# Macaron layer on one core: new call sequences on all engines before and after the loop over the attention units

## What is computed

```python
x = x + 0.5 * ffn(layernorm(x))
x = x + attention(layernorm(x))
x = x + 0.5 * ffn(layernorm(x))
```

```python
logits = flat @ router_w.T
_, topk_idx = top_k(logits + router_bias, 4)
topk_w = softmax(logits) at topk_idx, divided by its sum
y = einsum(silu(xg @ gate) * (xg @ up), down)     # xg: the tokens of each expert
out = zeros.at[tok_table].add(y * w_table)        # scatter-add
out = out + shared experts of flat
```

```python
q, k, v = x @ (codes * scales) + bias
attn = softmax(q @ k.T / sqrt(128))
out = (attn @ v) @ (wo_codes * wo_scales) + bo
```

## Time and profile before

| what | us |
|---|---|
| median of 3 runs | 972.84 (972.01 to 973.99) |
| profiled execution | 972.94 |
| its span, first to last instruction | 971.2 |
| PE matmul busy | 915.0 (94%) |
| VectorE busy | 763.6 (79%) |
| ScalarE busy | 646.6 (67%) |
| GpSimd busy | 645.6 (66%) |
| mean granted TensorE clock | 0.988 |

### The profile page before, as it was taken

One profiled execution on the slowest core, in us unless ns is written; L12 is line 12 of the kernel. 1 busy time (PEld: TensorE's weight loads), 2 busy tenths in 40 slices (PEclk: granted clock), 3 DMA queues, 4 the chain that ended last, 5 costly groups with the idle time before them and its releaser, 6 DMA issues.

```text
span 971.2 us, 18502 instructions
## 1 busy us (share of the span) xinstructions
PE 915.0 (94%) x5770; PEld 561.1 (58%) x5772; DVE 763.6 (79%) x2079; ACT 646.6 (67%) x1426; POOL 645.6 (66%) x607
## 2 busy tenths in 40 slices
PE   4999789999999999999999999999999999978987
PEld 3766466555555555555555555555555555765666
DVE  6954399998888888888888888888878789876247
ACT  5634446877778687777778778777777787543431
POOL 3368778878676868778676766867677455236741
PEclk9999989999999999999999999999999999988999
DMA  8979745666765868797785766756575564485757
GB/s 338 356 247 316 270 163 163 100 136 109 153 129 101 169 151 185 141 223 158 177 192 98 153 104 137 153 103 140 107 151 96 90 120 87 89 334 153 250 204 273
DMA packets 302978, 165.58 MB, mean 170 GB/s; under 512 B 278176, under 2 KB 285600, under 8 KB 300832
## 3 DMA queue, kind: packets, MB, share of 16 engines
q1 hardware_dynamic: 297696, 146.56, 62.7%
q0 software_dynamic: 3072, 9.44, 3.0%
q10 hardware_dynamic: 2112, 8.39, 2.1%
HBM read 68.93 MB, written 28.31 MB: 100 GB/s over the span
## 4 chain that ended last, share of the span: by engine, by line
PE 75%; DVE 13%; DMA 4%; issue 3%; ACT 2%; SPq 1%; another core or an unknown queue 0%; POOL 0%; DVEq 0%; ACTq 0%
PE b_p L110 5%; PE b_o L110 5%; PE b_o L111 5%; PE b_o L112 5%; PE b_p L111 5%; PE b_p L112 5%; PE b_s L110 5%; PE b_s L112 5%; PE b_s L111 5%; PE b_out L110 3%; PE b_out L112 3%; PE b_out L111 3%; PE b_v L110 2%; PE b_v L112 2%; PE b_v L111 2%
## 5 line engine op out<-in xcount | busy, mean ns | idle before, releaser
L2452 POOL TENSOR_TENSOR h<-pr,h 128x512 f16<-128x512 f32 x256 | 293.1, 1158 | 160.6 <-ACT h L1171 155.1
L1161 ACT ACTIVATE pr<-b_s,nmax,kappa 128x512 f32<-128x512 f32 x256 | 197.5, 774 | 41.1 <-DVE nmax L1907 36.7
L1904 DVE TENSOR_SCALAR_CACHE_REDUCE junk<-b_s 128x512 bf16<-128x512 f32 x256 | 175.3, 685 | 22.6 <-PE b_s L112 17.5
L1171 ACT ACTIVATE h<-pr 128x512 f16<-128x512 f32 x256 | 153.3, 626 | 0.7 <-DMA pT<-h 0.4
L1935 DVE SCALAR_TENSOR_TENSOR x<-b_out,rinv,x 128x256 f32<-128x256 f32 x256 | 111.4, 476 | 41.8 <-PE b_out L112 40.3
L110 PE MATMUL b_p<-xh,w 128*128 128x512 f16 x256 | 97.8, 382 | 3.1 <-DVE qT L1846 2.2
L110 PE MATMUL b_o<-pT,v 128*128 128x512 f16 x256 | 97.1, 379 | 1.7 <-DVE oT L1923 1.7
L111 PE MATMUL b_p<-xh,w 128*128 128x512 f16 x256 | 97.8, 382 | 0.0
L110 PE MATMUL b_s<-kT,qT 128*128 128x512 f16 x256 | 97.1, 379 | 0.7 <-ACT pr L1161 0.7
L112 PE MATMUL b_p<-xh,w 128*128 128x512 f16 x256 | 97.6, 381 | 0.0
L111 PE MATMUL b_s<-kT,qT 128*128 128x512 f16 x256 | 97.1, 379 | 0.0
(11 more groups left out here) (223 smaller groups left out, 2234.1 us busy)
## 6 DMA issues: line engine op xcount, KB each, us to landing
raw<-in_experts SPq DMA_DIRECT2D x32, 768.0 KB, 8.0
raw_cs<-in_heads SPq DMA_DIRECT2D x16, 1024.0 KB, 5.2
zrows<-zero ACTq DMA_DIRECT2D x4, 2048.0 KB, 11.5
z<-zrows SPq DMA_DIRECT2D x16, 512.0 KB, 4.2
zrows<-zero SPq DMA_DIRECT2D x16, 512.0 KB, 3.9
zl<-zrows SPq DMA_DIRECT2D x16, 512.0 KB, 8.8
rows<-xn SPq DMA_DIRECT2D x8, 512.0 KB, 10.7
pT<-h SPq DMA_TRANSPOSE x256, 3.2
```

Of the source, the lines that this page charges most:

```text
L1161: act.activation(pr[n % 4][:], b_s[n % 3][:], ACT.Exp, bias=nmax[:, u % 2, i:i + 1], scale=kappa[:, s:s + 1], accum_out=rsum[:, u % 2, i:i ...
L1171: act.activation(h[n % 4][:, 0, :], pr[n % 4][:], ACT.Copy).then_inc(q["p_high"], 1)
L1904: dve.tensor_scalar(junk[n % 2][:], b_s[n % 3][:], 0.0, None, ALU.add, ALU.max, accum_out=peaks[:, n % 2:n % 2 + 1]).then_inc(q["peak_read ...
L2452: pool.tensor_tensor(h[n % 4][:, 1, :], pr[n % 4][:], h[n % 4][:, 0, :], ALU.subtract).then_inc(q["p_split"], 1)
```

## The change

The function bodies, their waits, the buffers and the work are the same. Only the lists of calls change, on all five engines, before the loop and after it; the loops stay as they are. Every call of before is there once, in another place of the list. The diff has some 2,150 lines; these are the parts that the prediction speaks of.

ACT, start of the program (`job(j)` makes the high part of the router's, gate, up and down weights; `zero_out` issues a DMA of 2 MB of zeros):

```diff
             job(0)
             normalise(0)
+            normalise(1)
+            zero_out(0)
+            high(0)
             job(1)
-            high(0)
-            normalise(1)
+            job(2)
+            job(3)
             logits_out(0)
-            job(2)
             normalise(2)
+            normalise(3)
             high(1)
-            zero_out(0)
-            job(3)
-            normalise(3)
             high(2)
+            zero_out(1)
```

SP, start:

```diff
             load_x(0)
             load_x(1)
+            load_x(2)
+            load_qk_bias()
             load_router()
+            load_x(3)
+            load_gate()
             load_up()
-            load_x(2)
-            load_gate()
-            load_x(3)
+            load(0)
             load_down()
-            load(0)
-            load_qk_bias()
-            load_out_bias()
             load(1)
             load(2)
-            load(3)
-            load(4)
             store_rows(0)
             store_rows(1)
             store_rows(2)
             load_qk(0)
+            load(3)
+            load(4)
```

DVE, end of lap 0 (the combines; `scales(0)` and `statistics(4)` lead to the attention):

```diff
             hidden(11)
+            add_shared(1)
             combine(0)
+            combine(1)
             hidden(12)
-            scales(0)
-            combine(1)
             combine(2)
             combine(3)
+            combine(4)
+            scales(0)
             statistics(4)
+            add_shared(2)
             hidden(13)
+            combine(5)
             shift(4)
-            combine(4)
-            combine(5)
+            combine(6)
+            combine(7)
+            statistics(5)
             low(4)
             hidden(14)
-            add_shared(2)
             hidden(15)
-            combine(6)
+            keys_of(0)
             queries(0)
-            keys_of(0)
-            combine(7)
-            statistics(5)
+            shift(5)
             maxima(0, 0)
+            values(0)
```

POOL, the same place:

```diff
             range_weights(0, 2)
+            high_weights(0, 2)
+            power(4)
+            combine(8)
+            low_weights(0, 2)
+            hidden_low(12)
+            hidden_low(13)
+            power(5)
             range_weights(0, 3)
-            high_weights(0, 2)
-            low_weights(0, 2)
+            combine(9)
+            hidden_low(14)
             high_weights(0, 3)
+            hidden_low(15)
             low_weights(0, 3)
-            power(4)
+            combine(10)
...
             scale_weights(1, 0)
             scale_weights(1, 1)
-            hidden_low(12)
-            hidden_low(13)
-            combine(8)
-            hidden_low(14)
-            hidden_low(15)
-            combine(9)
-            combine(10)
-            power(5)
```

```diff
             load_z(28)
             load_z(29)
             load_z(30)
+            load_z(31)
             store_x(0)
-            load_z(31)
             store_x(1)
```

1155 lines of the change are left out of this document (576 added, 579 removed).

## The result

| kernel | median us | runs | ratio to before | granted clock, profiled run |
|---|---|---|---|---|
| before | 973.06 (972.01 to 974.39) | 8 | | 0.988 |
| changed | 980.25 (976.83 to 985.77) | 8 | 1.0077 [1.0051, 1.0103] | 0.992 |

The changed kernel is slower by 0.77%, 7.2 us, and outside the range on record (965.0 to 975.5). Its runs lie in three clusters, 976.8 to 978.4, 979.7 to 980.8 and 985.5 to 985.8. They go with the granted clock of the whole run: 0.992, 0.987 and 0.979. A straight line through the 8 runs gives 972.5 us plus 0.62 times the lost clock (one minus the clock, times the time), and leaves 0.5 us. The profiled run is the fastest of them, 976.83 (span 975.1), 3.9 us over the profiled run of before. So its trace shows about half of the loss, at a clock (0.992) that is even above that of before's profile (0.988); the rest must be read from other runs.

What follows compares the result with a forecast made beforehand. PE was taken to bound the loop, leaving at most the other 400 us to move. Terms +0.9 + 0 − 2.1 − 1.5 + 0 − 0.3 = −3.0 took 972.94 to 969.9 us; range 965.0 to 975.5.

Steps and rivals of the forecast that it cites:

- What bounds the kernel: PE bounds the loop from 250 to 800 us; the change leaves it alone, so at most the other 400 us move.
- A: Start up to the first logits: later down weights delay `logits_out(0)`, less `low_job(3)` taken off DVE's path; +0.9 us.
- B: Experts of both laps: same work in nearly the same order; 0 us, ends ±1.5.
- C: Combine stage: DVE's combines clear of POOL, first scores at 147.4 against 149.5; −2.1 us, ends −6 and +1.
- some 1.3 of collisions: Within the combine stage: time that `combine(6)` and `combine(7)` lose beside POOL, on top of their 3.1 us.
- 3 x 1.3: Combine stage: PE's `keys_of(0)`, `queries(0)` and `keys_of(1)`, 1.3 us each, ahead of the first scores.
- turns reversed: Rival: at the combines, DVE's steps wait for POOL's and `low(4)` ends near 149.7; total 976.4 us, chance 0.20.
- D: Units 1 to 8: DVE enters some 5 us earlier, PE's 3.5 idle us the ceiling; −1.5 us, ends 0 and −3.5.
- E: Units 57 to 63 and lap-1 routers: DVE's savings are waited away; 0 us, ends −2.2 and +1.2.
- F: Tail: `load_z(31)` issued one store earlier; −0.3 us, ends −1 and 0.
- lock rule: DVE and POOL lock their shared port for whole instructions; `combine(5)` and `combine(8)` then run one after the other, 4.3 us.

Runs made afterwards that it cites:

- only_units: The kernel before with the new order from `combine(0)` to unit 7 alone: 977.03 us, 1.0026 of before.
- turns_only: The kernel before with only DVE's and POOL's turns at the combines new, units 1 to 7 as before: 975.40 us, 1.0004 of before.
- Only_end: The kernel before with the new order only behind the loop: 974.57 us, 0.9993 of before.
- only_start: The kernel before with the new order only up to the first experts: 975.16 us, 1.0005 of before.
- before again: The kernel before, unchanged, run again for a second profile: 973.91 us, 0.9987 of before.

## Why the prediction was wrong

**What bounds the kernel**: right. The loop moved by 0.2 us of PE work, and everything happened in the other 400 us.

**A, the start** (+0.9 at the mask and experts, bounds -0.9 to +2.2): right in mechanism. The forecast had `logits_out(0)` at up to 19.9, it came at 19.66, and what it waited for is the down weights, as written. At the mask of chunk 3 it was +1.34, as the `low_job(3)` removed from that path gave back 0.6 and not 1.2. The down weights took 12.2 us to land and not 10.1, with `load(0)` ahead on SP's queue and the zeros of ACT's queue beside. *DMA: Bandwidth & Descriptors* of the Trainium skill, "Issuing engines are not separate DMA queues", says that DMAs of different engines run on the same 16 DMA engines and interleave. The longer landing fits that, but does not show it: no run parts the zeros from `load(0)`, whose 1.9 us by themselves would nearly do.

**B, the experts** (0): right alone (0.9992); +0.4 in the profile.

**C, the combine stage** (-2.1): wrong in sign. It measured +1.1 us in the profile (+2.7 at the scores of unit 0, of which 1.6 was already there at `combine(0)`). `statistics(4)`, `gate_up(14)`, the turn and `shift(4)` came within 0.6 us of the forecast once the 0.9 of the start is added. Two steps failed. One is "some 1.3 of collisions": `combine(6)` and `(7)` lost 2.8 us, so the low part of chunk 4 ended at 146.0 (143.5 plus 0.9 expected). The other is "3 x 1.3": PE's three calls up to the scores were taken at full clock, and took 6.05 us, from 146.17 to 152.22, as the clock was halved for 3.4 of them. The rival "turns reversed" named this place and these collisions; it put the bound at 145.6. It had 0.20, and the median is above even its 976.4. It did not name the clock or the units behind, so it would have been right in part only.

**D, units 1 to 8** (-1.5, bounds -3.5 to 0): the largest miss. It measured +2.1 us in the profile, outside my bounds; by the times of only_units and turns_only, 1.0026 and 1.0004, it is about 2.1 us as well. I had priced it as PE's idle time, a ceiling of 3.5 us that could only shrink, and had put a loss at nothing without a reason. PE's idle time grew to 5.25 us, nearly all of the growth at `values(3)`, and the clock was halved behind that wait. I had not asked what POOL's combines would then stand beside: `combine(14)` stood beside `scales_qk(1)` before, now `combine(13)` does too, and the chain became 1.0 us longer. Nor had I asked what PE has to do while it waits: two `scores` less. turns_only, which leaves this stretch as before, has no loss that can be told.

**E and F** (0 and -0.3): right in size. From unit 55 to `gate_up(31)` the gap fell by 0.4 us, with `shift(11)` and the mask at 0.16 and 0.42 us as forecast, though the turn of chunk 11 came 1.4 us later against unit 55 and not 0.1 to 0.6. From there to the end it fell by 0.5, as the last load's wait at PE's final sums fell. The two lines, of before and of the changed kernel:

```profile
956.11 1.10 PE L389 MATMUL tb<-zl,twice 128*128 128x256 f32 x4 [0.89 <-DMA zl<-zrows]
```

```profile
959.98 1.32 PE L389 MATMUL tb<-zl,twice 128*128 128x256 f32 x5 [0.22 <-DMA zl<-zrows]
```

**The clock** was no term of the sum, and it should have been. Taking 0.6 us per microsecond of lost clock, the slope of the changed kernel's runs, it is at equal clock about 4 us slower than before (972.7 against 968.6 on the chip where both were run again), and its lower clock (0.987 against 0.990 in the medians) adds some 1.8 us; between its own best and worst runs the clock makes 7 to 8 us. The slope is rough: over the other kernels it lies between 0 and 0.9. Of the lock rule of *SBUF — State Buffer* in the Trainium skill ("SBUF: two separate sides"), the trace again shows the kind: a step of 0.16 us waits up to 1.07 us beside a POOL operation of 1.26. The 4.3 us that the prediction gave `combine(5)` and `combine(8)` by that rule came out at 3.6, from 133.28 to 136.85: the two overlap in part.

**What stays open.** The parts measured alone add up to 1.5 us by the ratios, 3 by the medians, on the faster chips; the whole gave 7.2 and 5.9. The clock explains some 2 of these; whether the rest is start and units working together was not measured on the faster chips. A part of it may lie behind the loop: the second profile of the changed kernel on a faster chip is only 0.5 us behind the second one of before at unit 55 and 4.3 at the end, with 17 us at half clock in the second feed-forward layer against 6.8. Only_end shows no such loss, so the new end alone does not make it. On the slower chips the loss of start and units is there (1.0 to 1.6 and 2.4 to 3.0 us), and the new experts and end together gain 3.8 us, which they do not on the faster ones (0.9992 and 0.9993); most of that gain goes with a higher granted clock, 0.981 against 0.975 in the medians. Why, no run shows.

## What to carry to other kernels

When operations of two engines that stretch each other are moved apart, list what each of them is moved *beside*, and price the small steps of a serial chain first: here each stretched from 0.16 us to as much as one operation of the other engine, 0.7 to 1.2. Give a term that can only gain by your sum a loss side too. A late wait is rarely removed by moving one call; see in the trace which call then waits for the moved one. And where single waits grow on an engine whose clock is granted, put the half-clock stretch behind them into the sum, and time enough runs to see it. Take two profiles of the same kernel before reading a difference of 2 us between two points.

## What the runs showed of the hardware

TensorE's clock fell to its lower level, 1.2 GHz, at the 3.2 us wait at `values(3)` in all eight profiles that have this wait (for 3.4 us each time, from between 0.2 us before the wait's end and 1.1 us behind it), and behind the 1.5 us wait at the same place in none of eight. Behind waits of 2.0 to 2.7 us it fell in some profiles (only_start at 220.48, before at 147.81) and not in others (before again at 147.66 and 219.14). So it also fell behind the waits at the combines, but not in every profile of the same kernel, and the runs of one kernel lie up to 10 us apart, mostly for it. In the first experts it fell for 10 to 14 us in seven of the thirteen profiles with the new order there, six of the seven on the slower chips, and in none of the seven with the old order, none of which was taken on those chips; so order and chip can't be told apart here.

Small VectorE steps of 0.16 us took up to 1.23 us beside a GpSimd operation, of combines and `probs_low` alike, and 0.15 to 0.17 us with GpSimd idle.

Chips of the same type were 28 us apart for the same kernel. Between two profiles of the changed kernel 12.2 us of this lie ahead of `combine(0)`, 16.0 behind unit 55 and less than 1 us between; the granted clock was lower too, 0.974 against 0.992, which at 0.6 us per microsecond of lost clock would be an estimated 11 us of it.
